# A selective-scan block with its mixed output layer: softplus bursts moved in half of the blocks, filler matmuls in the head, four C products moved from VectorE to GpSimd

## What is computed

```
x_ = in_proj(ctx); u = silu(conv4(x_) + conv_b)             # 512 channels x 512 positions
dt_low, B, C = x_proj(u); dt = softplus(dt_proj(dt_low) + dt_proj_b)
for t in range(512):                                        # for each channel d and state n
    state = state * exp(dt[t] * A) + (dt[t] * u[t]) * B[t]
    y[t]  = sum_n state[n] * C[t, n]
x = x + ((y + D * u) * silu(layernorm(x))).T
x = x + layernorm(x) @ sum_r(factors[r]) / sqrt(8) + bias
```

## Time and profile before

| | |
|---|---|
| median of three runs | 483.33 us (483.25 to 483.36) |
| profiled execution | 482.48 us, span 480.7 us |
| busy: DVE, PE, POOL, ACT | 453.5, 432.1, 420.6, 344.7 us |
| mean granted clock of TensorE | 0.989 |
| DMA | 53.96 MB, mean 112 GB/s |

### The profile page before, as it was taken

One profiled execution on the slowest core, in us unless ns is written; L12 is line 12 of the kernel. 1 busy time (PEld: TensorE's weight loads), 2 busy tenths in 40 slices (PEclk: granted clock), 3 DMA queues, 4 the chain that ended last, 5 costly groups with the idle time before them and its releaser, 6 DMA issues.

```text
span 480.7 us, 4118 instructions
## 1 busy us (share of the span) xinstructions
PE 432.1 (90%) x1119; PEld 185.3 (39%) x1119; DVE 453.5 (94%) x327; ACT 344.7 (72%) x578; POOL 420.6 (88%) x223
## 2 busy tenths in 40 slices
PE   8799797999979868898989789899979999989996
PEld 5134343434434233333434244343434343344432
DVE  5797999989999999989999999999999899999996
ACT  4669574977659788796869977697879876654422
POOL 4369999998979899997999979797998958999972
PEclk9989999999999989999999999999999999999999
DMA  5799746438982000100694000000396000000002
GB/s 193 267 355 350 200 80 138 83 55 217 292 337 88 1 0 0 42 25 1 191 412 168 0 22 1 0 24 0 132 381 237 1 22 23 22 22 22 0 1 88
DMA packets 16847, 53.96 MB, mean 112 GB/s; under 512 B 1828, under 2 KB 2084, under 8 KB 15800
## 3 DMA queue, kind: packets, MB, share of 16 engines
q1 hardware_dynamic: 15384, 45.14, 25.9%
q0 software_dynamic: 1152, 8.39, 8.8%
q10 hardware_dynamic: 288, 0.18, 0.1%
HBM read 49.24 MB, written 4.46 MB: 112 GB/s over the span
## 4 chain that ended last, share of the span: by engine, by line
POOL 53%; issue 20%; DVE 11%; ACT 6%; PE 4%; DMA 4%; SPq 1%; POOLq 0%; DVEq 0%; ACTq 0%
POOL h L1093 40%; POOL h L1086 9%; DVE dA L946 7%; POOL dtu L1079 3%; DMA c_rep<-bc_scratch 2%; PE y L519 2%; DVE acc L920 2%; ACT dA L776 1%; DMA chan<-channel 1%; DVE h L952 1%; PE work L415 1%; POOL fsum L1123 1%; DVE h L946 1%; ACT gate L690 0%; SPq L331 0%
## 5 line engine op out<-in xcount | busy, mean ns | idle before, releaser
L1093 POOL TENSOR_TENSOR h<-b_rep,dtu 128x1024 f32<-128x1024 f32 x127 | 302.3, 2446 | 12.3 <-DMA b_rep<-bc_scratch 11.3
L519 PE MATMUL y<-h,ident 128*128 128x512 f32 x508 | 236.5, 602 | 34.9 <-DVE h L952 33.0
L946 DVE TENSOR_TENSOR_SCAN dA<-dA,h 128x1024 f32<-128x1024 f32 x97 | 221.8, 2287 | 11.6 <-ACT dA L776 11.1
L776 ACT ACTIVATE dA<-dt,a_neg 128x512 f32<-128x512 f32 x256 | 166.0, 681 | 92.9 <-DVE h L952 76.2
L519 PEld LDWEIGHTS y<-h,ident 128*128 128x128 f32 x508 | 92.8, 190 | 166.2 <-issue 103.7
L952 DVE TENSOR_TENSOR h<-dA,c_rep 128x1024 f32<-128x1024 f32 x96 | 117.1, 1220 | 2.4 <-DMA c_rep<-bc_scratch 0.3
L1086 POOL TENSOR_TENSOR h<-h,c_rep 128x1024 f32<-128x1024 f32 x31 | 74.5, 2403 | 22.3 <-DVE h L946 22.3
L946 DVE TENSOR_TENSOR_SCAN h<-dA,h 128x1024 f32<-128x1024 f32 x31 | 70.6, 2279 | 0.1
L403 PE MATMUL work<-ctx_sb,w_in 128*128 128x512 f32 x60 | 30.6, 644 | 0.3 <-DMA w_in<-w_inT 0.2
L507 PE MATMUL work<-fsum,xnT 128*128 128x512 f32 x64 | 28.8, 592 | 0.0
L920 DVE SCALAR_TENSOR_TENSOR acc<-work,chan,acc 128x511 f32<-128x511 f32 (+2 forms) x30 | 21.6, 731 | 1.3 <-ACT acc L655 1.2
(11 more groups left out here) (128 smaller groups left out, 375.3 us busy)
## 6 DMA issues: line engine op xcount, KB each, us to landing
b_rep<-bc_scratch SPq DMA_DIRECT2D x32, 512.0 KB, 9.7
c_rep<-bc_scratch SPq DMA_DIRECT2D x32, 512.0 KB, 9.3
fsum<-factors POOLq DMA_DIRECT2D x8, 1024.0 KB, 8.3
x<-x SPq DMA_DIRECT2D x4, 1024.0 KB, 7.7
out<-x SPq DMA_DIRECT2D x16, 256.0 KB, 2.0
ctx_sb<-ctxT SPq DMA_DIRECT2D x3, 512.0 KB, 5.7
ctx_sb<-ctxT SPq DMA_DIRECT2D x2, 256.0 KB, 4.4
w_in<-w_inT SPq DMA_DIRECT2D x1, 384.0 KB, 5.2
```

The costliest lines, as they stand in the source:

```text
L519: mm = pe.matmul(y[:], ident[:], h[:, (s * PAIRS + j) % H_RING, i, :], start=False, stop=(j == sum_order(s)[-1] and i == 1))
L776: act.activation(dA[:, j % 2, i, :], dt[:, k % 2, :], ACT.Exp, scale=a_neg[:, k, 2 * j + i:2 * j + i + 1]).then_inc(exp_done, 1)
L946: dve.tensor_tensor_scan(pair if on_pool(s * PAIRS + j) else decay, decay, pair, 0.0, ALU.mult, ALU.add).then_inc(scanned, 1)
L1093: pool.tensor_tensor(h[:, (s * PAIRS + j) % H_RING], b_rep[:, j], dtu[:, k % 2, :].unsqueeze(1).to_broadcast([P, 2, L]), ALU.mult).then_in ...
```

## The change

`SOFTPLUS_SLOT = 2` becomes `SOFTPLUS_SLOTS = (0, 2, 0, 2)`, by k: in the eight blocks with k = 0 or 2 the softplus burst stands behind the decays of pair 0. `FIRST_FILL` puts 6, 0, 2 and 2 small matmuls (zeros times ones, into a part of `dA` that is not yet in use) ahead of the four matmuls of `x_proj(0)` and 3 ahead of `dt_proj(0)`. `POOL_C` gets four pairs more: pair 2 of block 3 and pair 4 of blocks 9, 11 and 13.

```diff
-POOL_C = ((0, 4), (0,), (0, 2), (0,), (0, 2), (0, 2), (0, 2), (0, 2, 4), (0, 2), (0, 2), (0, 2), (0, 2), (0, 2), (0, 2),
-          (0, 2), (0, 2))
-SOFTPLUS_SLOT = 2
+POOL_C = ((0, 4), (0,), (0, 2), (0, 2), (0, 2), (0, 2), (0, 2), (0, 2, 4), (0, 2), (0, 2, 4), (0, 2), (0, 2, 4), (0, 2),
+          (0, 2, 4), (0, 2), (0, 2))
+SOFTPLUS_SLOTS = (0, 2, 0, 2)
...
+FIRST_FILL = (6, 0, 2, 2, 3)
...
+            def fill_first(i):
+
+                for _ in range(FIRST_FILL[i]):
+                    pe.matmul(dA[:, 1, 1, :], still[:], ones[:], start=True, stop=True)
+
             def x_proj(b):
                 for k in range(KB):
                     if b == 0:
+                        fill_first(k)
                         pe.wait_ge(u_done, k + 1)
...
             x_proj(0)
+            fill_first(KB)
             pe.wait_ge(w_dt_landed, 16)
...
-                    if j == SOFTPLUS_SLOT and is_d:
+                    if j == SOFTPLUS_SLOTS[k] and is_d:
```

## The result

The changed kernel takes 485.55 us (median of seven, 485.36 to 487.15), the one before 483.33; the ratio is 1.0044 with a 95% interval of 1.0026 to 1.0061. It is slower by 2.2 us, where 2.0 was forecast (485.3); how much of that agreement is luck is said further down. The profiled execution took 485.50 us, span 483.7, 3.02 more than that of before.

What follows compares the result with a forecast made beforehand. DVE's queue plus the places where ACT is late bound most of the run; DVE and POOL run side by side late on. Terms summed to +1.96 us: 484.4 for the profiled execution, 485.3 median; range 479.6 to 487.2.

Steps and rivals of the forecast that it cites:

- A moved product is worth 1.27 us: Each C product moved to POOL saves DVE 1.27 us and costs POOL 2.31; block 3 -1.26, block 9 -0.84.
- Block 11's product is lost in block 12: ACT's pauseless stretch up to block 12's decays doesn't move when DVE saves; blocks 11 and 12 together +0.23 us.
- Block 13's product costs instead of paying: POOL has no gap behind its 5.00 us wait, so block 14's first scans come late: DVE about +2.2, not -1.27.
- block 14's burst adds to it: Burst behind late pair 0 delays pair 1's scan from 418.23 to 421.53: +3.30 us, containing the product's 2.2.
- The stall of 0.37 at pair 1: With the burst behind pair 0, pair 1's decays end 0.37 us after DVE wants them in block 2; likewise blocks 4, 12.
- The stall of 3.1: By the Trainium skill's page, with a 1.38 us drain per switch, the stall at pair 1 instead of 0.37; left out.
- The gains in blocks 6 and 10: With no burst behind pair 2, the wait in front of pair 5 shrinks: -0.42 us and -0.44 us.
- The head, +1.5: Block 0: the new burst waits for `dt_proj(1)` until 27.07, delaying the tap and later work: +1.5 us.
- The clock stays up with the fillers: Head: fillers close most PE pauses, granted clock 1.0 from 21 to 28 us, eight matmuls 3.59 us, not 6.31.
- Rival 2: Whole kernel: DVE alone is the bound, so what is taken from it is gained; -3.5 us, 479.8; chance 0.26.

Runs made afterwards that it cites:

- No fillers: The changed kernel without the thirteen fillers of the head (FIRST_FILL all zeros): 488.34 us, ratio 1.0086 against the kernel before.

## Why the prediction came out right, point by point

- *A moved product is worth 1.27 us where DVE binds alone.* Right in block 3 and again in block 1. In block 9 it gave 0.82, as forecast, since ACT is late behind it (0.63 to 0.83 in the other runs, apart from the one called "No fillers").
- *Block 11's product is lost in block 12.* Right, and shown by the run with that one burst put back. The term was +0.04, not +0.23. I took the decays of block 12's pair 0 to be fixed by PE. But ACT ran them at 357.17 before, 0.1 us behind the end of a product of DVE that they wait for (355.85 + 1.22 = 357.07); with DVE out of the way they come 0.22 us earlier. The line is from the kernel before:

```profile
355.85 1.22 DVE L952 TENSOR_TENSOR h<-dA,c_rep 128x1024 f32<-128x1024 f32 x1
```

- *Block 13's product costs instead of paying, and block 14's burst adds to it.* Right: 3.27 against 3.30, in two parts. The product costs 2.3 where no burst stands behind it (the run with the products alone), the burst 1.0 where no product does (two runs). This is what decides the sign; without the two the changed kernel is 3 us faster, as fast as before or a little faster.
- *The stall of 0.37 at pair 1 in blocks 2 and 4.* Right: the shift rises by 0.38 there. The stall of 3.1 that was set beside it doesn't appear.
- *The gains in blocks 6 and 10.* Sized wrong: 0.15 and 0.16 in place of 0.42 and 0.44. I let the decays of pair 3 start when DVE's product was done. Ahead of them ACT has a copy of PE's result (L764 before), which the burst had hidden; the copy now waits, and this is ACT's row in block 6:

```profile
201.56 0.60 ACT L772 ACTIVATE x<-work 128x512 f32<-128x512 f32 x1 [3.05 <-PE work L516]
```

- *The head, +1.5.* Right in kind, a little too small: +2.07 and +1.65 in the two profiles, and +1.65 to +4.1 in all six with this burst and the fillers. Much of that spread arises ahead of anything that was changed: the last four matmuls of the very first `in_proj` start at 10.31 to 11.60 us (10.43 before). Counted from there, the head is +1.75 to +1.77 in all five in which the clock stayed up around the second `in_proj`. Of the 0.26 over my 1.5, 0.1 is a later start of the second `in_proj` than I had worked out, and 0.1 its eight matmuls of 3.70 us in place of 3.59. Their weights explain little of the spread: they land 5.0 to 5.4 us after their issue in every profile. The first twelve matmuls take 5.39 us in the second profile and 6.45 in the run with block 12's burst put back; why is not shown.
- *The clock stays up with the fillers.* Mostly: it fell between 21 and 28 us in 2 of the 10 profiles with fillers and in 2 of the 3 without. Three are too few to call this shown. What the profiles do show is what a fall costs: with the burst waiting for `dt_proj(1)`, the head (counted as above) is +3.3 and +3.5 in the two profiles where the clock fell for 3.4 us, 1.6 to 1.7 more than where it stayed up; with the burst behind pair 2, the kernel before, where it fell for 6.8 us, is only 0.2 to 0.3 us behind the run with the fillers alone.
- *The time.* Near, and in part by luck. The sum said +1.96 for the profiled execution, and the two profiles gave +3.02 and +2.59; in the first, the head is 0.6 worse than forecast, and blocks 6 and 10 together 0.5. The median still came to 485.55 against 485.3, because I had added the 0.85 us by which the profile of the kernel before lies under its median. The profiles of the changed kernel lie only 0.05 and 0.2 under theirs, so one error covered most of the other.
- *My range.* 479.6 to 487.2 is 7.6 us wide, so that it holds the time says little; the terms are the test. Rival 2, for which it had to be so wide, fails mostly on POOL in block 13. It also took block 14's burst to cost 0.37 without the product; it costs 1.0.

## What to carry to other kernels

An engine that is busy for 94% of the span is not one bound but a chain of places, and each edit has to be priced at the place where it is made: the same product moved off the busiest engine gave 1.27 us, nothing, or cost 2.2 us, by whether another engine had a lead there. For a moved instruction, read the lead of the receiving engine (how long its result had been ready when it was used) up to the next point where it waits anyway. A burst put into a pause is free only if the instruction ahead of it is on time, too.

## What was not expected of the hardware

- TensorE's granted clock falls at other places in each execution (50 to 57, 172 to 176, 275 to 279 and 415 to 419 us in the first profile after, 21.7 to 28.5 and 172 to 175 before). Mostly this costs nothing, though PE is 90% busy; in one execution it cost DVE 2.0 us by the end of block 9, through a copy of ACT that waited for PE.
- A small instruction of DVE can wait for a long one of POOL. The TENSOR_SCALAR of 128 x 4 (L1012) took 0.17 us with POOL idle (before). In eleven profiles it started in the middle of a B product of POOL; there it took 0.48 to 1.63 us, and ended 0.02 to 0.03 us after POOL's instruction each time. DVE's scans and C products show nothing of the kind (means of 2.29 and 1.22 us in both kernels, with POOL busy for 88 and 89% of the span).
- Behind the head, the same program repeats to some hundredths of a microsecond: blocks 1 to 12 of the changed kernel's two profiles differ by 0.05 us in any term. Between the profiles of all runs the rest of the difference is the head (shifts of -0.4 to +4.1, by kernel and by execution) and a fall of the clock. Whether that also makes the spread of the kernel before, 482.6 to 487.3 us in one job, is not shown: it has one profile.
